# Attention in a transformer kernel on Trainium2: the order in which own and context keys are projected, and the block's order on every engine

## The chip, the cores and the metric

One core of one Trainium2 chip. The metric is the device time of one execution in microseconds (us), slowest core, lower is better. Differences of about 0.3% are the least that a measurement of this kernel tells from none.

## The reference, cut to what matters

The whole program is a two-layer transformer: cross attention, feed-forward, cross attention, feed-forward. The change touches the first attention only. For 8 batches of 256 positions:

```
xn = layernorm(x)                                  # 512 wide
q  = rms_norm(xn @ wq)      -> 16 heads of 128, rotated (rope)
k  = rms_norm(xn @ wk)      ->  4 key heads of 128, rotated
kc = rms_norm(ctx @ wk_ctx) ->  4 key heads of 128, not rotated
v  = xn @ wv ; vc = ctx @ wv_ctx
p  = softmax(q . [kc ; k] / sqrt(128), causal on the own part)
x  = x + (p . [vc ; v]) @ wo
```

Each key head serves 4 query heads. "Own" keys and values come from x, "context" ones from ctx_2048.

## The kernel before, in words

Attention is 64 blocks (`NBLK`). Block i is batch i // 8, key head i // 2 % 4 and query tile i % 2 (128 rows): 4 query heads against 384 keys in an even block and 512 in an odd one (256 of the context and the own ones up to the diagonal). So each key head is a pair of an even and an odd block, and each batch is 8 blocks. Numbers are kept to fp32 accuracy by splitting them into a high and a low plane (`kT[0]`, `kT[1]`; `planes[:,0]`, `planes[:,1]`) and by three products of planes.

Keys and values are made in 64 units, one per block, two blocks ahead: block i projects unit i + 2. A unit is either own or context for one key head (`unit`, L125). In the kernel before, apart from the first pair, the context unit is the even one and the own unit the odd one. The projection lands in a PSUM bank (`kv_bank`: `quad[:, 3]` for even units, `bK` for odd ones) and its keys go round the engines:

- own unit: PE projects (`pe_kv`, L393) -> ACT copies the raw keys out (`act_k_raw`, L592) and sums their squares (`act_k_sq`, L584) -> POOL rotates them (`pool_k_rope`, L1066 to L1068, `pool_k_add`, L1074) and takes the root (`pool_rs`, L1059) -> ACT scales (`act_k_scale`, L600) -> PE transposes back into the same bank (`pe_k_turn`, L405) -> ACT writes the high plane (`act_k_hi`, L624) -> DVE the low plane (`dve_k_lo`, L837) -> the scores of the next pair may start (`pe_s`, L449 to L451, waits for `kt_lo` at head 0).
- context unit: the same without the rotation; ACT scales straight out of the bank (`act_k_n`, L661), L626 and L839 write the planes.
- values: `act_v_hi` (L635) and `dve_v_lo` (L848), one block later.

Five instruction streams are written out by hand, and every engine runs its own list strictly in order: `pe_step`, `act_step`, `dve_step`, `pool_step` and the SP queue's loop in `sp_program`. Semaphores (`wait_ge`) tie them. There is no planner; the order within a block is what these functions say. In a block before:

- PE: scores of heads 0, 1; projection of unit i + 2 (24 matmuls); scores of heads 2, 3; transposed queries of block i + 1 (`pe_q_turn`, L433); queries of block i + 2 (12 matmuls, L421); probabilities times values of block i - 1 in three parts (`pe_pv`, L479), with `pe_k_turn(i + 2)` among them.
- DVE: per head the masked scores (`dve_ev`, L904) and the low plane of the probabilities (`dve_p_lo`, L891); the reciprocal of the sums (`dve_ri`, L912, twice); `dve_o_lo` (L939), `dve_v_lo`, `dve_q_lo` (L884), and at the end `dve_k_lo(i + 2)` and the rotation of the queries `dve_q(i + 2)` (L876 to L878).
- ACT: the exponentials (`act_exp`, L687, and a small scaling L692 after each second one), `act_q_sq` (L645), `act_q_hi` (L653) and the steps of the units above.
- POOL: the high plane of the probabilities (`pool_norm`, L1087, four times), `pool_q_add` (L1080), the steps of the units.
- SP: the transposing DMAs of the probability planes (L302), the store of the output.

Once per batch new input is brought in ("the turn", block i % 8 == 6): the context tiles are split (`act_c_hi`, L566, `act_c_square`, L667, `pool_c_lo`, L1046; at the end of block 4 of the batch), x is loaded (`sp_x`, L244), its statistics taken (`dve_ln_a`, L812 to L816, at the end of block 5), rooted (`pool_ln_rs`, L1052), applied (`dve_ln_b`, L822), transposed (`pe_x_turn`, L353) and split (`act_x_hi`, L574, `dve_x_lo`, L828), all three in block 6.

## Time and profile before

| | |
|---|---|
| median of 3 runs | 1596.91 us (1596.77 to 1601.76) |
| the profiled execution | 1596.18 us, of which its span 1594.9 us |
| attention's blocks in the trace | 27 to 905 us |
| mean granted TensorE clock | 0.964 of full speed |
| busy share of the span | PE 90%, DVE 72%, ACT 61%, POOL 45% |

Engines: PE is TensorE, PEld its weight loads, DVE VectorE, ACT ScalarE, POOL GpSimd, SP the DMA queue's engine. L405 is line 405 of the kernel. `out<-in` are the tiles that an instruction writes and reads. A wait "A <- B" is time in which A sat idle until B released it. An instruction that follows another on its engine often starts a little before the other's shown end, so steps are counted from start to start.

### The profile page before, as it was taken

To read this page: it belongs to the slowest core of one execution; us is meant where nothing else is said; L and a number is where in the kernel's file an instruction comes from. 1 tells how busy PE (TensorE), PEld (TensorE's weight loads), DVE (VectorE), ACT (ScalarE), POOL (GpSimd) and SP (SyncE) were. 2 spreads that over 40 slices of the span, in tenths; PEclk is the share of its full clock that TensorE was granted. 3 is DMA by queue.
4 is the path that set the end of the run, shared out by engine and by line. 5 is a ranking of instruction groups with operands and counts; after the bars stand their busy time and mean duration, and the time that the engine had idled before them with its cause. 6 is when DMAs were issued, how large, how long until landed. Compare 5 with 4: busy or idle time off the path is not lost. (4 is left out here: it accounts for less than half of the span.)

```text
span 1594.9 us, 24891 instructions
## 1 busy us (share of the span) xinstructions
PE 1429.5 (90%) x7820; PEld 1046.0 (66%) x7820; DVE 1156.2 (72%) x2836; ACT 975.1 (61%) x2647; POOL 716.1 (45%) x809
## 2 busy tenths in 40 slices
PE   7888989888979898889888789999998899999988
PEld 5665767666767676667676456666666566666653
DVE  5677776767767777777778875655566888888774
ACT  6565665666656656666565674555554666667655
POOL 5456464555554655655655600000003455555444
PEclk9789999999999999999998989999999999999999
DMA  7334555545545555555488998878885401111000
GB/s 282 70 83 118 119 126 115 114 113 124 125 120 114 125 115 117 115 123 126 106 203 202 255 308 276 287 248 256 267 264 161 151 21 47 54 54 41 28 14 27
DMA packets 321892, 223.76 MB, mean 140 GB/s; under 512 B 276960, under 2 KB 277088, under 8 KB 320352
## 3 DMA queue, kind: packets, MB, share of 16 engines
q1 hardware_dynamic: 321760, 222.16, 52.4%
q8 instruction: 63, 1.03, 0.3%
q14 instruction: 69, 0.57, 0.1%
HBM read 113.05 MB, written 41.94 MB: 97 GB/s over the span
## 5 line engine op out<-in xcount | busy, mean ns | idle before, releaser
L891 DVE SCALAR_TENSOR_TENSOR planes<-E,small,planes 128x384 f16<-128x384 f32 (+1 forms) x256 | 210.8, 843 | 70.5 <-POOL planes L1087 69.0
L1087 POOL TENSOR_SCALAR planes<-E,small 128x384 f16<-128x384 f32 (+1 forms) x256 | 160.0, 637 | 159.1 <-DVE small L912 151.7
L421 PE MATMUL bank<-wq,xT 128*128 128x512 f32 x768 | 199.6, 409 | 9.3 <-ACT wq L559 9.1
L687 ACT ACTIVATE E<-E,small 128x384 f32<-128x384 f32 (+1 forms) x256 | 170.8, 675 | 51.1 <-DVE small L904 51.0
L904 DVE CUSTOM_DVE_ANT_0 E<-quad,mask,small 128x384 f32<-128x384 f32 (+1 forms) x256 | 169.2, 677 | 44.7 <-PE quad L451 44.6
L1300 PE MATMUL bank<-wq,ot 128*128 128x512 f32 x768 | 187.6, 403 | 9.9 <-DMA ot<-ot_scratch 5.6
L479 PE MATMUL bank<-PT,vv 128*128 128x512 f16 x672 | 177.9, 401 | 0.0
L1300 PEld LDWEIGHTS bank<-wq,ot 128*128 128x128 f32 x768 | 147.8, 193 | 44.3 <-DMA ot<-ot_scratch 6.1
L421 PEld LDWEIGHTS bank<-wq,xT 128*128 128x128 f32 x768 | 143.4, 194 | 39.2 <-issue 9.3
L1080 POOL TENSOR_TENSOR t<-t 128x512 f32<-128x512 f32 x64 | 84.7, 1324 | 172.3 <-DVE t L878 172.3
L1596 POOL TENSOR_TENSOR cl<-cl,fixed 128x1 f32<-128x1 f32 x16 | 8.8, 550 | 279.5 <-DVE cl L1480 279.5
L449 PE MATMUL quad<-kT,qT 128*128 128x384 f32 (+1 forms) x256 | 107.8, 421 | 26.9 <-DVE kT L837 23.6
L2482 POOL TENSOR_TENSOR bhw<-bh,lnw 128x512 f32<-128x512 f32 x64 | 81.7, 1277 | 82.0 <-DVE bh L2270 81.9
L479 PEld LDWEIGHTS bank<-PT,vv 128*128 128x128 f16 x672 | 63.0, 101 | 71.4 <-issue 24.2
L393 PEld LDWEIGHTS quad<-wkc,cT 128*128 128x128 f32 x720 | 99.1, 209 | 0.0
L393 PE MATMUL quad<-wkc,cT 128*128 128x256 f32 x720 | 99.0, 298 | 0.0
L451 PE MATMUL quad<-kT,qT 128*128 128x384 f32 (+1 forms) x256 | 97.4, 381 | 0.0
L450 PE MATMUL quad<-kT,qT 128*128 128x384 f32 (+1 forms) x256 | 97.4, 380 | 0.0
L393 PEld LDWEIGHTS bank<-wkv,xT 128*128 128x128 f32 x744 | 93.4, 189 | 2.5
L1059 POOL TENSOR_TENSOR small<-small,fixed 128x6 f32<-128x6 f32 (+2 forms) x65 | 89.0, 1370 | 12.3 <-ACT small L611 12.3
L393 PE MATMUL bank<-wkv,xT 128*128 128x256 f32 x744 | 94.3, 283 | 0.0
L645 ACT ACTIVATE junk_sq<-bank 128x128 bf16<-128x128 f32 x256 | 67.4, 279 | 37.2 <-DVE t L878 37.0
(313 smaller groups left out, 3304.1 us busy)
## 6 DMA issues: line engine op xcount, KB each, us to landing
ot_scratch<-OT SPq DMA_DIRECT2D x64, 512.0 KB, 2.7
ot<-ot_scratch SPq DMA_DIRECT2D x64, 512.0 KB, 5.3
wkv_f<-in_w SPq DMA_DIRECT2D x12, 512.0 KB, 5.0
wkc_f<-in_w SPq DMA_DIRECT2D x12, 512.0 KB, 6.3
wkv_f<-in_wg SPq DMA_DIRECT2D x11, 512.0 KB, 6.8
wkv_f<-in_wd SPq DMA_DIRECT2D x11, 512.0 KB, 6.9
wkv_f<-in_wu SPq DMA_DIRECT2D x10, 512.0 KB, 7.1
stg<-in_ctxT SPq DMA_DIRECT2D x16, 256.0 KB, 3.0
```

Source lines behind the costliest of these rows:

```text
L393: ins = pe.matmul(kv_bank(u)[:, t * 256:t * 256 + 256], src[i][:, k, t * 128:t * 128 + 128], w[j][:, g, k, :], start=(n == 0), stop=(n == 11))
L421: ins = pe.matmul(bQ[:], xT[p][:, k, qt * 128:qt * 128 + 128], wq[j][:, g, k, :], start=(part == 0 and k == 0), stop=(part == 2 and k == 3))
L449: pe.matmul(bank[:, 0:n], qh, kh, start=True, stop=False)
L450: pe.matmul(bank[:, 0:n], ql, kh, start=False, stop=False)
L451: pe.matmul(bank[:, 0:n], qh, kl, start=False, stop=True).then_inc(f["s_mm"], 1)
L479: ins = pe.matmul(bO[:].rearrange("p (h q) -> p h q", h=4), vv[:, x, i // 2 % 2, kt, :], heads[:, y, :, kt, :], start=(part == 0 and kt == ...
L687: act.activation(p, p, ACT.Exp, bias=nm[:, i % 2, h:h + 1], scale=-1.0, accum_out=sm[:, i % 2, h:h + 1]).then_inc(f["s_exp"], 1)
L891: dve.scalar_tensor_tensor(plane(i, 1, h), E[:, h, 0:width(i)], ri[:, i % 2, h:h + 1], plane(i, 0, h), ALU.mult, ALU.subtract).then_inc(f[ ...
L904: dve.tensor_tensor_reduce(E[:, h, 0:n], bank_s(i, h)[:, 0:n], mask[:, 512 - n:512], scale=rs6[:, (i + 1) % 2, 2 + h:3 + h], scalar=3.0e38 ...
L1059: pool.tensor_tensor(rs6[:, e % 2, c], ve6[:, c], half[:, c], ALU.pow).then_inc(f["n_rs"], 1)
L1087: pool.tensor_scalar(plane(i, 0, h), E[:, h, 0:width(i)], ri[:, i % 2, h:h + 1], 1.0, ALU.mult, ALU.mult).then_inc(f["p_n"], 1)
L1300: ins = pe.matmul(y_bank(n)[:], ot[:, c % 4, i, k * 128:k * 128 + 128].bitcast(F32R), wo[j][:, g, k, :], start=(g == 0 and k == 0 and q == ...
```

## The change

Units: in all batches the own unit is now the even one (projected in even blocks) and the context unit the odd one, except for the first key head of batches 1 to 7, whose own unit needs the new x and stays odd (`unit`). `own_before` counts own units, since they no longer alternate. The own unit's second half of the work (`act_k_scale`, `pe_k_turn`, `act_k_hi`, `dve_k_lo`, and `act_v_hi`, `dve_v_lo`) moves from its own block to the next, odd one, and stands there right behind the scores of heads 2 and 3. In odd blocks the context unit's `pe_k_turn` follows the first part of `pe_pv`. On DVE `dve_q(i + 2)` and, in odd blocks, `dve_k_lo(i + 2)` stand ahead of `dve_p_lo(i, 3)`. At the turn, the statistics of x move from block 5 to block 6, the split of the context from the end of block 4 to the middle of block 5, x's loads from block 4 to block 5, and in block 7 the projection comes ahead of all scores. The weights of groups 1 to 3 are loaded and split with the own ones first. No arithmetic is added or taken away.

```diff
--- before.py
+++ after.py
@@ -125,18 +125,22 @@
     def unit(u):
 
 
-        bg, own = divmod(u, 2)
-        return bg, 1 - own if bg == 0 else own
+        bg, n = divmod(u, 2)
+        return bg, n if bg and bg % 4 == 0 else 1 - n
+
+    def own_before(u):
+
+        return sum(unit(w)[1] for w in range(u))
 
     def piece_of(p):
 
 
-        g, j = divmod(p, 4)
-        return g, (j + 1) % 4 if g == 0 else j
+        g, n = divmod(p, 4)
+        return g, ((1, 0, 2, 3) if g else (1, 2, 3, 0))[n]
 
     def pieces(g, j):
 
-        return 4 * g + (j - 1) % 4 + 1 if g == 0 else 4 * g + j + 1
+        return 4 * g + ((1, 0, 2, 3) if g else (1, 2, 3, 0)).index(j) + 1
 
     def piece(p):
 
@@ -314,7 +318,7 @@
         sp_w(0, "wkc")
         sp.dma_start(mask[:], a["mask"]).then_inc(f["mask_in"], 16)
         for g in range(1, 4):
-            for src in ("wkc", "wkv", "wq"):
+            for src in ("wkv", "wkc", "wq"):
                 sp_w(g, src)
         sp_c(2)
         sp_c(3)
@@ -330,14 +334,13 @@
                     for x in range(2):
                         sp_p_turn(i, half, x)
                         sp_last(i, 1 + 2 * half + x)
+                        if b + 1 < NB and r == 5 and half != x:
+                            sp_x(2 * b + 2 + half)
             elif i == NBLK:
                 sp_last(i, 4)
             if b + 1 < NB and r == 6:
                 sp_c(2 * b + 4)
                 sp_c(2 * b + 5)
-            if b + 1 < NB and r == 4:
-                sp_x(2 * b + 2)
-                sp_x(2 * b + 3)
 
 
 
@@ -495,22 +498,29 @@
 
     def pe_step(i):
         turn = i % 8 == 6 and i + 2 < NBLK
+        ahead = i % 8 == 7
+        if ahead:
+            pe_kv(i + 2, 0)
+            pe_kv(i + 2, 1)
         pe_s(i, 0)
         pe_s(i, 1)
         if i == 0:
             pe_q(1, 2)
-        pe_kv(i + 2, 0)
-        pe_kv(i + 2, 1)
+        if not ahead:
+            pe_kv(i + 2, 0)
+            pe_kv(i + 2, 1)
+        pe_s(i, 2)
+        pe_s(i, 3)
+        if i % 2:
+            pe_k_turn(i + 1)
         if turn:
+            for part in range(3):
+                pe_pv(i - 1, part)
             pe_x_turn(2 * (i // 8) + 2)
             pe_x_turn(2 * (i // 8) + 3)
-        pe_s(i, 2)
-        pe_s(i, 3)
-        if turn:
-            pe_pv(i - 1, 0)
-            pe_pv(i - 1, 1)
+            pe_scale(i)
         pe_q_turn(i + 1)
-        if scaled(i):
+        if scaled(i) and not turn:
             pe_scale(i)
         if i == 60:
             pe_w1_sum()
@@ -520,12 +530,10 @@
             ffn["pe_y"](0, 1)
         if not turn:
             pe_pv(i - 1, 0)
-            if i % 2 == 0:
-                pe_pv(i - 1, 1)
-        pe_k_turn(i + 2)
-        if i % 2:
+            if i % 2:
+                pe_k_turn(i + 2)
             pe_pv(i - 1, 1)
-        pe_pv(i - 1, 2)
+            pe_pv(i - 1, 2)
         if i == 62:
             pe.wait_ge(f["q_sq"], NBLK)
             ffn["pe_y"](0, 0)
@@ -562,7 +570,7 @@
         b, t = divmod(c, 2)
         sem, n = c_in(c)
         act.wait_ge(sem, n)
-        after(act, f["kv_mm"], 8 * b - 1)
+        after(act, f["kv_mm"], 8 * b)
         act.copy(cT[0][:, :, t * 128:t * 128 + 128],
                  stg[:, c % 2, :].rearrange("p (k n) -> p k n", k=4)).then_inc(f["c_hi"], 1)
 
@@ -589,12 +597,13 @@
             return
         act.wait_ge(f["kv_mm"], u + 1)
         after(act, f["kt_mm"], u)
+        after(act, f["k_rope"], own_before(u))
         act.copy(kn, kv4(u)[:, 0]).then_inc(f["k_raw"], 1)
 
     def act_k_scale(u):
         if u >= NU or not unit(u)[1]:
             return
-        act.wait_ge(f["k_rope"], u // 2 + 1)
+        act.wait_ge(f["k_rope"], own_before(u) + 1)
         act.wait_ge(f["n_rs"], u + 1)
         for t in range(2):
             ins = act.activation(ka[:, t], ka[:, t], ACT.Copy, scale=rs6[:, u % 2, t:t + 1])
@@ -656,7 +665,8 @@
         if u >= NU or unit(u)[1]:
             return
         act.wait_ge(f["n_rs"], u + 1)
-        after(act, f["kt_mm"], u)
+        after(act, f["k_rope"], own_before(u))
+        after(act, f["kt_mm"], u - unit(u - 1)[1])
         for t in range(2):
             ins = act.activation(kn[:, t], kv4(u)[:, 0, t], ACT.Copy, scale=rs6[:, u % 2, t:t + 1])
         ins.then_inc(f["k_n"], 1)
@@ -722,21 +732,30 @@
         if i == 0:
             act_w_hi(6)
         act_o(i - 2)
+        if i % 2 == 0 and i:
+            act_v_hi(i + 1)
         if i:
-            act_v_hi(i + 1)
             act_q_sq(i + 1)
         if 1 <= i <= 4:
             act_w_hi(2 * i + 6)
+        if i % 8 == 7:
+            act_k_raw(i + 2)
         act_exp(i, 0)
         act_exp(i, 1)
         if i == 0:
             act_q_sq(1)
-        act_k_raw(i + 2)
+        if i % 2:
+            act_k_scale(i + 1)
+        if i % 8 != 7:
+            act_k_raw(i + 2)
         act_k_sq(i + 2)
         act_ve(i + 2)
-        if turn:
-            act_x_hi(2 * (i // 8) + 2)
-            act_x_hi(2 * (i // 8) + 3)
+        if i % 8 == 5 and i + 3 < NBLK:
+            for m in (2 * (i // 8) + 2, 2 * (i // 8) + 3):
+                act_c_hi(m)
+                act_c_square(m)
+        if i % 2:
+            act_k_hi(i + 1)
         act_last(i, 0)
         act_exp(i, 2)
         act_k_n(i + 2)
@@ -745,18 +764,21 @@
             act_w_hi(7)
         elif i <= 4:
             act_w_hi(2 * i + 7)
+        if turn:
+            act_x_hi(2 * (i // 8) + 2)
+            act_x_hi(2 * (i // 8) + 3)
+        if i % 2:
+            act_v_hi(i + 1)
         act_q_hi(i + 1)
         if i == 0:
             act_v_hi(0)
             act_v_hi(1)
-        act_k_scale(i + 2)
-        act_k_hi(i + 2)
+        if i % 2:
+            if i % 8 == 7:
+                act_k_scale(i + 2)
+            act_k_hi(i + 2)
         if i in (1, 3):
             act_w_square(2 + i // 2)
-        if i % 8 == 4 and i + 4 < NBLK:
-            for m in (2 * (i // 8) + 2, 2 * (i // 8) + 3):
-                act_c_hi(m)
-                act_c_square(m)
         act_last(i, 1)
         act_last(i, 2)
 
@@ -947,35 +969,38 @@
             dve_w(5)
             dve_q(1)
         if turn:
+            dve_ln_a(2 * (i // 8) + 2)
+            dve_ln_a(2 * (i // 8) + 3)
+        dve_o_lo(i - 2)
+        if i % 2 == 0 and i:
+            dve_v_lo(i + 1)
+        dve_ri(i, 0)
+        if turn:
             dve_ln_b(2 * (i // 8) + 2)
             dve_ln_b(2 * (i // 8) + 3)
-        dve_o_lo(i - 2)
-        if i:
-            dve_v_lo(i + 1)
-        dve_ri(i, 0)
         if i == 0:
             dve_w(6)
         dve_last(i, 0)
         dve_ev(i, 2)
+        if i % 2:
+            dve_k_lo(i + 1)
+        dve_p_lo(i, 0)
+        dve_ev(i, 3)
+        dve_p_lo(i, 1)
+        if i % 2:
+            dve_v_lo(i + 1)
+        if 1 <= i <= 4:
+            dve_w(2 * i + 6)
+        dve_ri(i, 1)
         if turn:
             dve_x_lo(2 * (i // 8) + 2)
             dve_x_lo(2 * (i // 8) + 3)
-        dve_p_lo(i, 0)
-        dve_ev(i, 3)
         if scaled(i):
             dve_scale(i)
-        dve_p_lo(i, 1)
-        if 1 <= i <= 4:
-            dve_w(2 * i + 6)
-        dve_ri(i, 1)
         dve_q_lo(i + 1)
         if i == 0:
             dve_w(7)
         dve_p_lo(i, 2)
-        dve_p_lo(i, 3)
-        if i % 8 == 5 and i + 3 < NBLK:
-            dve_ln_a(2 * (i // 8) + 2)
-            dve_ln_a(2 * (i // 8) + 3)
         if scaled(i):
             dve_unscale(i)
         if i == 0:
@@ -983,11 +1008,13 @@
             dve_v_lo(1)
         if 1 <= i <= 4:
             dve_w(2 * i + 7)
-        dve_k_lo(i + 2)
+        dve_q(i + 2)
+        if i % 2:
+            dve_k_lo(i + 2)
+        dve_p_lo(i, 3)
         if i == 16:
             dve_co()
         dve_last(i, 1)
-        dve_q(i + 2)
 
     def dve_co():
 
@@ -1061,8 +1088,7 @@
     def pool_k_rope(u):
         if u >= NU or not unit(u)[1]:
             return
-        pool.wait_ge(f["k_raw"], u // 2 + 1)
-        after(pool, f["k_rope"], u // 2)
+        pool.wait_ge(f["k_raw"], own_before(u) + 1)
         pool.tensor_tensor(kb[:, :, 0:64], kn[:, :, 64:128], tab[:, 3, :, 0:64], ALU.mult)
         pool.tensor_tensor(kb[:, :, 64:128], kn[:, :, 0:64], tab[:, 3, :, 64:128], ALU.mult)
         g_.did(pool.tensor_tensor(ka, kn, tab[:, 2, :, :], ALU.mult))
@@ -1105,24 +1131,33 @@
         pool.tensor_tensor(lo, loaded, hi.bitcast(F32), ALU.subtract).then_inc(f["wo_lo"], 1)
 
     def pool_step(i):
+        turn = i % 8 == 6 and i + 2 < NBLK
         pool_q_add(i + 1)
+        if i % 8 == 7:
+            pool_k_rope(i + 2)
         pool_norm(i, 0)
         pool_norm(i, 1)
-        pool_k_rope(i + 2)
+        if turn:
+            pool_ln_rs(2 * (i // 8) + 2)
+            pool_ln_rs(2 * (i // 8) + 3)
+        if i % 8 != 7:
+            pool_k_rope(i + 2)
         pool_rs(i + 2)
-        pool_k_add(i + 2)
-        if scaled(i):
+        if i % 8 == 7:
+            pool_k_add(i + 2)
+        if i % 8 == 5 and i + 3 < NBLK:
+            pool_c_lo(2 * (i // 8) + 2)
+            pool_c_lo(2 * (i // 8) + 3)
+        if scaled(i) and not turn:
             pool_scale(i)
         pool_norm(i, 2)
         pool_norm(i, 3)
+        if scaled(i) and turn:
+            pool_scale(i)
+        if i % 8 != 7:
+            pool_k_add(i + 2)
         if i >= 57:
             pool_wo(i - 57)
-        if i % 8 == 4 and i + 4 < NBLK:
-            pool_c_lo(2 * (i // 8) + 2)
-            pool_c_lo(2 * (i // 8) + 3)
-        if i % 8 == 5 and i + 3 < NBLK:
-            pool_ln_rs(2 * (i // 8) + 2)
-            pool_ln_rs(2 * (i // 8) + 3)
 
     def pool_program():
         pool_ln_rs(0)
```

## Rows read from the trace of the kernel before

**Rows 1.** The waits of the whole program: who waited for whom, us in total, times, longest.

```profile
PE bank L405 <- ACT kk L600: 79.4, 31, 4.4
...
PE quad L449 <- DVE kT L837: 23.6, 25, 2.5
```

**Rows 2.** Windows: length, busy of PE, PEld, DVE, ACT, POOL (instructions), PEclk, DMA share, GB/s.

```profile
398.88:409.80 10.92, 10.91 (x66) 8.93 (x67) 7.77 (x20) 7.14 (x29) 4.88 (x6) 1.00 0.55 129
409.80:423.43 13.63, 11.60 (x66) 8.73 (x64) 10.15 (x23) 8.67 (x31) 8.44 (x10) 1.00 0.48 110
434.36:451.54 17.18, 11.61 (x66) 8.74 (x64) 12.51 (x29) 11.02 (x38) 11.82 (x14) 1.00 0.61 141
558.97:586.58 27.61, 24.69 (x145) 19.47 (x146) 20.84 (x50) 16.16 (x60) 15.93 (x21) 0.98 0.48 110
480.64:506.32 25.68, 23.66 (x130) 18.78 (x130) 18.06 (x43) 16.25 (x60) 13.35 (x16) 0.95 0.53 113
```

**Rows 3.** Timeline (start us, us, engine, line, operation, count) of PE, block 27.

```profile
411.38 3.04 PE L393 MATMUL bank<-wkv,xT 128*128 128x256 f32 x24
...
415.64 0.60 PE L433 MATMUL bank<-fixed,t 128*128 128x128 f32 x4
...
418.85 0.82 PE L479 MATMUL bank<-PT,vv 128*128 128x512 f16 x3
421.28 0.44 PE L405 MATMUL bank<-fixed,kk 128*128 128x128 f32 x2 [1.61 <-ACT kk L600]
```

**Rows 4.** Timeline of ACT in block 27.

```profile
410.77 0.47 ACT L635 ACTIVATE vv<-quad,small 128x256 f16<-128x256 f32 x1
...
418.14 0.20 ACT L692 ACTIVATE small<-small 128x2 f32<-128x2 f32 x1
...
421.76 0.37 ACT L624 CAST kT<-bank 128x256 fp32r<-128x256 f32 x1 [0.53 <-PE bank L405]
```

**Rows 5.** Timeline of DVE in block 27 and at the start of block 28.

```profile
410.23 0.68 DVE L876 TENSOR_TENSOR t<-bank,tab 128x512 f32<-128x512 f32 x1
...
411.49 0.74 DVE L904 CUSTOM_DVE_ANT_0 E<-quad,mask,small 128x512 f32<-128x512 f32 x1
...
415.84 0.75 DVE L891 SCALAR_TENSOR_TENSOR planes<-E,small,planes 128x512 f16<-128x512 f32 x1
...
418.38 0.17 DVE L912 RECIPROCAL small<-small 128x2 f32<-128x2 f32 x1 [0.46 <-ACT small L692]
...
421.20 1.83 DVE L891 SCALAR_TENSOR_TENSOR planes<-E,small,planes 128x512 f16<-128x512 f32 x2 [1.66 <-POOL planes L1087]
422.96 0.41 DVE L837 TENSOR_TENSOR kT<-bank,kT 128x256 fp32r<-128x256 f32 x1
423.30 0.68 DVE L876 TENSOR_TENSOR t<-bank,tab 128x512 f32<-128x512 f32 x1
```

**Rows 6.** Timeline of POOL in block 27.

```profile
420.49 1.35 POOL L1087 TENSOR_SCALAR planes<-E,small 128x512 f16<-128x512 f32 x2
```

**Rows 7.** Timeline of ACT at the start of block 29 and in block 30.

```profile
434.26 0.61 ACT L566 CAST cT<-stg 128x512 fp32r<-128x512 f32 x1
...
436.80 0.67 ACT L699 ACTIVATE OT<-bank,cl 128x512 fp32r<-128x512 f32 x1
...
458.05 1.05 ACT L574 CAST xT<-bank 128x512 fp32r<-128x512 f32 x2
```

**Rows 8.** Timeline of DVE at the end of block 29 and in block 30.

```profile
449.06 0.68 DVE L812 BATCH_NORM_STATS2 small<-stg 128x6 f32<-128x512 f32 x1
...
451.07 0.41 DVE L837 TENSOR_TENSOR kT<-bank,kT 128x256 fp32r<-128x256 f32 x1
...
453.73 1.11 DVE L822 TENSOR_SCALAR stg<-stg,small 128x512 f32<-128x512 f32 x2
...
459.22 1.28 DVE L828 TENSOR_TENSOR xT<-bank,xT 128x512 fp32r<-128x512 f32 x2
```

**Rows 9.** Timeline of POOL at the end of block 29.

```profile
451.23 0.56 POOL L1052 TENSOR_TENSOR small<-small,fixed 128x1 f32<-128x1 f32 x1 [0.44 <-DVE small L816]
```

## The prediction

> **What bounds the kernel now.** The busy shares name PE (90%), so the first view to read is what PE waits for [rows 1]. Two rows carry the attention stage: 31 waits for the scaled own keys (ACT L600), 79.4 us together, and 25 waits of the scores for the keys' low plane (DVE L837), 23.6 us. Both belong to the own unit, whose keys go through all four engines in the last block before they are needed. The windows [rows 2] show where: block 26 (even) takes 10.92 us with PE busy 10.91, block 27 (odd) 13.63 us with PE busy 11.60. Even blocks are bound by PE, odd ones by the keys' chain. Block 29, before the turn, takes 17.18 us at the same PE work. The turn's pair, 38 and 39, takes 27.61 us. So about 103 us could go, if nothing took the waits' place. Whether something does is read in the order of DVE and ACT in an odd block, since every engine keeps its list.
>
> Below, times in block 27 count from its first score at 409.80.
>
> **Even blocks.** The two transposes of a unit's keys leave PE (0.44 us long after a stall [rows 3]; I take 0.25 of PE's time), and PE has no gap to fill: 10.67 us instead of 10.92. POOL gets the rotation there, some 2.5 us before the high planes of heads 2 and 3. That makes the block's last low planes later, but the next block's scores don't wait for them, and the transposing DMAs have most of a block of slack. I cost it at nothing; if that cover went, the next masking would start late.
>
> **Odd blocks, the chain as it will be.** What was at the end is now in the middle.
> - PE's own-key transposes stand where the queries' stood, at 415.64, which is 5.84. From such a transpose to the high plane's copy takes 0.48 (421.28 to 421.76 [rows 3, 4]): 6.32. The copy is 0.37, with a handover of 0.04: DVE's low plane starts at 6.73 and holds DVE for 0.34 (422.96 to 423.30 [rows 5]): 7.07.
> - Only then comes the low plane of head 0, which stood at 415.84, i.e. 6.04 [rows 5]. It, the masking of head 3, its exponential and the scaling L692 behind it are now 1.03 later: L692 at 8.34 [rows 4] goes to 9.37.
> - Before, the reciprocal followed L692 at once (418.38, 8.58 [rows 5]). Now DVE's list has the values' low plane first, and that waits for ACT's high plane, which stands behind L692: 0.1, a copy of 0.47 [rows 4] with 0.04, and 0.39 of DVE (its twin on the keys is 0.41 long). That is 1.0: reciprocal at 10.37.
> - POOL's high planes of heads 2 and 3 follow 0.26 later, 10.63; before, they were held back by the rotation until 420.49, 10.69 [rows 6]. So all that the rotation's departure frees is used up by the two inserted steps.
> - Low plane of head 2 after 0.71 (420.49 to 421.20): 11.34. The two low planes took 1.76 until the keys' one began [rows 5]; a lone one is 0.75 long, 0.67 from start to start, so the first took 1.09. Next 12.43.
> - Then the queries' rotation, 1.26 (410.23 to 411.49 [rows 5]), and now the context keys' low plane at 13.69. From there to the next score 0.47 (422.96 to 423.43): **14.16** against 13.63.
>
> PE meanwhile is done at about 11.5 (its work from 418.85 on, 9.05, is nine matmuls and two transposes, 2.3 us). Its two waits have become one of 2.6 us at the first score of the next pair. The context unit's transposes find their keys ready. Sum of a plain pair: +0.53 - 0.25 = +0.28 us.
>
> **Block 29 and its like (six of them).** The statistics leave the end of DVE's list, 2.0 us straight ahead of the keys (449.06 to 451.07 [rows 8]). The context's four ACT operations, 2.54 us (434.26 to 436.80 [rows 7]), now stand ahead of the own keys' high plane: they start at about 5.5 and end at 8.05 where 6.32 was possible, +1.73. Block: 14.16 + 1.73 = 15.9 against 17.18. With the even one -1.5 us per pair.
>
> **The turn (seven).** In block 30 DVE now takes the statistics (2.0) where it took the normalisation (1.11 [rows 8]). Its first reciprocal comes at about 5.0. POOL does two high planes (1.4 with the start), then the roots of 0.56 [rows 9], DVE the normalisation from 7.0 to 8.05, and only then the masking of head 2. The exponentials of heads 2 and 3, behind it, are through at about 10.6 (estimate: 2.5 us after the masking, as there is one low plane and one exponential between). ACT's high planes of x follow them (two in 1.05 [rows 7]) and DVE's low ones (1.28 [rows 8]): 12.5. PE must have these before the queries' transposes, since they share a bank, and it runs out of other work at 9.5: the 10.67 of an even block, less the 3.2 of the queries (415.64 to 418.85 [rows 3]), and 2.2 for x and the scales (24.69 of PE in the turn's pair, 22.51 in blocks 26 and 27 [rows 2]), make 9.6. That is a new stall of some 3.1 us. Transposes and queries (3.2) and the projection of block 31, now first, 2.9 (411.38 for 3.04, less its overlap [rows 3]), follow: scores of block 31 at 18.7. That block then walks like an odd one, except that the projection is done: it saves about 2.0, 12.2. Sum 30.9 against 27.61: +3.3 us.
>
> **Queues.** SP's loads of x stand behind the transposes of block 29; they arrive at about 2 us into block 30 (3.0 us after issue), and the second statistics want them at 2.9. Cover, narrow; a miss would add to the turn. The weight loads change places only; blocks 0 to 5 wait for `wq`, which doesn't move.
>
> **Sum.** Twelve plain pairs +3.4; six with the context's split -9.2; seven turns +23.1; the first three and last four pairs, whose extra work (weights, sums) I don't follow, at the plain price +2.0. Together +19.3 on the profiled execution's 1596.2: **1615.5 us**. That execution lies 0.7 below the median of 1596.9; I forecast 1615. Bounds of the unknowns: each odd block's chain holds some ten handovers, which I take to be right within 0.3 us, below or above: 32 times, 10 us. The turn's new stall lies between 0 (all of it hidden) and 4.5 (x late too).
>
> **A rule weighed.** POOL's root of the norms (L1059) and the low plane of head 0 will overlap at 7.1. In the Trainium skill, SBUF — State Buffer, "Who interferes with whom", a VectorE instruction with two SBUF inputs and a GpSimd one that reads SBUF block each other for a whole instruction. The 1.09 for the first low plane beside POOL's L1087 agrees with it. By the rule the overlap with L1059 would add 0.1 per odd block, 3 us in all; my sum leaves it out.
>
> **Rivals.**
> - *PE's clock falls in every odd block.* Now block 27 has 2.03 us of idle PE in two parts, the longer 1.61 [rows 2, 3], at clock 1.00. Pair 38 and 39 has 2.92 (27.61 less 24.69 busy), and pair 32 and 33, which also follows a turn, shows 0.95 and takes 25.68 instead of 24.55 [rows 2], +1.13. A single wait of 2.6 us lies nearer to 2.9 than to 1.6. If it falls after each of some 18 to 25 odd blocks: +20 to +28, about 1638. In the Trainium skill, TensorE: Matmul & The Clock Gate, "What's actually happening", the full clock is what recent activity earns, so a longer unbroken wait speaks against this change. Against it: the sum of idle time in a pair hardly changes. 0.15.
> - *The turn is hidden.* If x's planes are ready before PE runs dry, seven stalls of 3.1 us go: 1593.5. For it: ACT is busy for 16.16 of the turn's 27.61 us [rows 2], so there is room. Against: nothing in the new list lets x's high planes go ahead of the exponentials. 0.18; half of it would be measured as no change.
> - *Faster: the odd block is bound by PE.* Place: the reciprocal of heads 2 and 3 in an odd block. If it comes at 7.8 instead of 10.4, the low plane of the keys is done by 11.1 and PE goes on at 11.5: 2.6 us less in 18 odd blocks, 1568. It beats the kernel before as soon as the reciprocal comes before about 9.3, on the plain pairs and with the turn as costed. It would need the own keys' transposes ready to be subtracted before head 2 is masked, at 5.4; PE issues them at 5.84. 0.10, part of it at a smaller gain.
> - *The low plane of head 2 loses the 0.42 us that it spends beside POOL* (1.09 less 0.67), because the lists now meet elsewhere. Then 31 x 0.42 less: 1602. Against it: both high planes still follow each other on POOL there. 0.07.
>
> **From these to the numbers.** Forecast 0.50, the rest as above. Faster by over 0.3% (under 1592.1; 0.3% is about what a measurement of this kernel tells from no change): the PE-bound case and half of the hidden turn, 0.18. Within: the rest of the hidden turn and a little of the others, 0.15. Slower: 0.67. Range 1591 to 1636: it leaves out the PE-bound case, the lowest part of the hidden turn and the clock's worst, some 0.2. The forecast's own range is 1605 to 1625.
>
> **What will show it.** In the waits: "PE bank L405 <- ACT kk L600" down from 79.4 to under 25 (block 31's kind alone), and the scores' wait for the low plane up from 23.6 to 60 or 80, now with L839. In the windows: even blocks 10.7, odd ones 14.2, block 29's kind 15.9, the turn's pair near 31 with a gap of 3 us ahead of L433. In DVE's timeline of an odd block: a wait ahead of L848 and L912 at 10.4. PEclk 1.00 in plain pairs. I am wrong if odd blocks come out near 11.5 (the chain is shorter than walked), if the gap ahead of L433 is missing in the turn, or if plain pairs show a clock below 1.

## The result, and the profile after

The changed kernel takes 1656.91 us (median of four runs, 1655.94 to 1658.66), the kernel before 1598.06 in the same comparison (four runs): ratio 1.0366, 95% interval 1.0344 to 1.0387. That is some 59 us more where I forecast 18 more, above my range of 1591 to 1636. The direction was right, the size not.

Where the time is shows in one window for each kernel, from the start of the span to the first score of block 62. Columns as in [rows 2]. The kernel before, then the changed one:

```profile
0.00:888.07 888.07, 767.36 (x4222) 600.01 (x4222) 644.88 (x1461) 546.33 (x1960) 491.11 (x584) 0.95 0.56 131
```

```profile
0.00:946.79 946.79, 798.54 (x4223) 636.60 (x4223) 667.17 (x1463) 537.86 (x1960) 496.29 (x584) 0.91 0.51 122
```

Nearly all of the difference, 58.7 of the spans' 59.8 us, is in the attention stage. PE runs as many instructions (4222 and 4223) and is busy 31.2 us longer with them, at a granted clock that fell from 0.95 to 0.91. The rest, 27.5 us, is more idle time.

The waits of PE in the changed kernel, the counterparts of [rows 1] (its lines: scores L452 to L454, own-key transposes L408, queries' transposes L436):

```profile
PE quad L452 <- DVE kT L861: 83.1, 24, 5.8
...
PE bank L408 <- ACT kk L609: 26.6, 7, 3.8
...
PE bank L436 <- issue: 16.1, 7, 2.4
```

The first two rows moved as forecast, both a little further up than said: the wait for the scaled own keys fell from 79.4 to 26.6 (forecast "under 25"), the scores' wait rose from 23.6 to 83.1 ("60 or 80"), in longer single waits. The third is the new gap of the turn.

The windows of blocks 26, 27, 29, 30 and 31 of the changed kernel, as in [rows 2]:

```profile
426.08:438.30 12.22, 12.22 (x65) 10.19 (x65) 8.76 (x20) 6.21 (x26) 7.74 (x10) 0.86 0.43 102
438.30:452.45 14.15, 11.56 (x67) 9.01 (x66) 10.37 (x25) 9.37 (x34) 6.03 (x7) 1.00 0.52 117
464.66:481.07 16.41, 11.57 (x67) 9.01 (x65) 10.95 (x25) 11.53 (x40) 8.55 (x9) 1.00 0.52 118
481.07:502.22 21.15, 18.71 (x104) 16.24 (x105) 13.71 (x34) 9.25 (x38) 9.23 (x13) 0.84 0.36 81
502.22:516.11 13.89, 10.09 (x44) 6.34 (x42) 9.40 (x22) 6.60 (x22) 7.52 (x11) 0.85 0.55 142
```

The chain of the odd block, in DVE's timeline of block 27 (columns as in [rows 5]; the block's first score is at 438.30; L859 and L861 are the low planes of own and context keys, L913 the low planes of the probabilities, L898 to L900 the queries' rotation):

```profile
444.95 0.42 DVE L859 TENSOR_TENSOR kT<-quad,kT 128x256 fp32r<-128x256 f32 x1 [0.56 <-ACT kT L633]
...
448.19 0.48 DVE L870 SCALAR_TENSOR_TENSOR vv<-quad,small,vv 128x256 f16<-128x256 f32 x1 [0.82 <-ACT vv L644]
448.59 0.15 DVE L934 RECIPROCAL small<-small 128x2 f32<-128x2 f32 x1
...
449.57 1.17 DVE L913 SCALAR_TENSOR_TENSOR planes<-E,small,planes 128x512 f16<-128x512 f32 x1 [0.22 <-POOL planes L1113]
450.67 0.68 DVE L898 TENSOR_TENSOR t<-bank,tab 128x512 f32<-128x512 f32 x1
...
451.93 0.47 DVE L861 SCALAR_TENSOR_TENSOR kT<-bank,small,kT 128x256 fp32r<-128x256 f32 x1
452.32 1.60 DVE L913 SCALAR_TENSOR_TENSOR planes<-E,small,planes 128x512 f16<-128x512 f32 x1
```

Counted from 438.30: own keys' low plane 6.65 (walked 6.73), reciprocal 10.29 (10.37), low plane of head 2 at 11.27 (11.34), rotation 12.37 (12.43), context keys' low plane 13.63 (13.69). The waits in brackets are the two inserted steps: DVE waits for the own keys' high plane, and, ahead of the reciprocal, for the values' high plane. What the walk did not price is the last row: 1.60 us for an operation that takes 0.75 in [rows 5].

PE's side of the same block and of the turn:

```profile
452.45 0.45 PE L452 MATMUL quad<-kT,qT 128*128 128x384 f32 x1 [2.59 <-DVE kT L861]
...
494.54 0.78 PE L436 MATMUL bank<-fixed,t 128*128 128x128 f32 x4 [2.43 <-issue]
494.97 4.54 PE L424 MATMUL bank<-wq,xT 128*128 128x512 f32 x12
...
512.99 0.69 PE L408 MATMUL bank<-fixed,kk 128*128 128x128 f32 x2 [3.80 <-ACT kk L609]
```

There is one wait of 2.59 us at the scores, as walked (2.6), and the clock falls behind it: 1.00 in the window of block 27, 0.86 in those of the even blocks on either side. The queries' projection behind the turn's gap takes 4.54 us; in an odd block, at full clock, 2.98.

### The profile page after: what moved, and what is told of

Its sections match the earlier page's. It is cut to its first block and busy times, and to the rows that moved or that the text cites. A ratio compares the mean times of both kernels' runs of the same rounds, so it can differ in the third digit from the quotient of the medians.

```text
span 1654.7 us, 24817 instructions
## 1 busy us (share of the span) xinstructions
PE 1456.5 (88%) x7777; PEld 1082.5 (65%) x7820; DVE 1178.2 (71%) x2836; ACT 966.8 (58%) x2647; POOL 722.5 (44%) x809
## 5 line engine op out<-in xcount | busy, mean ns | idle before, releaser
L913 DVE SCALAR_TENSOR_TENSOR planes<-E,small,planes 128x384 f16<-128x384 f32 (+1 forms) x256 | 233.4, 912 | 17.9 <-POOL planes L1113 15.1
L424 PE MATMUL bank<-wq,xT 128*128 128x512 f32 x768 | 208.7, 423 | 10.4 <-ACT wq L567 6.8
L452 PE MATMUL quad<-kT,qT 128*128 128x384 f32 (+1 forms) x256 | 109.5, 428 | 84.2 <-DVE kT L861 83.1
L424 PEld LDWEIGHTS bank<-wq,xT 128*128 128x128 f32 x768 | 150.4, 203 | 41.9 <-issue 6.9
L482 PE MATMUL bank<-PT,vv 128*128 128x512 f16 x672 | 171.1, 397 | 2.2 <-DVE vv L870 2.2
L1106 POOL TENSOR_TENSOR t<-t 128x512 f32<-128x512 f32 x64 | 95.1, 1486 | 112.8 <-DVE t L900 112.8
L452 PEld LDWEIGHTS quad<-kT,qT 128*128 128x128 f32 x256 | 52.6, 205 | 108.7 <-DVE kT L861 95.4
L482 PEld LDWEIGHTS bank<-PT,vv 128*128 128x128 f16 x672 | 63.0, 102 | 81.0 <-issue 22.8
L709 ACT ACTIVATE OT<-bank,cl 128x512 fp32r<-128x512 f32 x64 | 44.1, 689 | 118.6 <-PE bank L482 110.5
L1086 POOL TENSOR_TENSOR small<-small,fixed 128x6 f32<-128x6 f32 (+2 forms) x65 | 98.8, 1520 | 7.3 <-ACT small L620 7.2
L454 PE MATMUL quad<-kT,qT 128*128 128x384 f32 (+1 forms) x256 | 101.9, 398 | 0.0
L453 PE MATMUL quad<-kT,qT 128*128 128x384 f32 (+1 forms) x256 | 101.5, 396 | 0.0
L396 PEld LDWEIGHTS quad<-wkv,xT 128*128 128x128 f32 x552 | 91.9, 249 | 0.0
L396 PE MATMUL quad<-wkv,xT 128*128 128x256 f32 x552 | 90.3, 334 | 0.0
```

The source lines that it names most:

```text
L396: ins = pe.matmul(kv_bank(u)[:, t * 256:t * 256 + 256], src[i][:, k, t * 128:t * 128 + 128], w[j][:, g, k, :], start=(n == 0), stop=(n == 11))
L424: ins = pe.matmul(bQ[:], xT[p][:, k, qt * 128:qt * 128 + 128], wq[j][:, g, k, :], start=(part == 0 and k == 0), stop=(part == 2 and k == 3))
L452: pe.matmul(bank[:, 0:n], qh, kh, start=True, stop=False)
L453: pe.matmul(bank[:, 0:n], ql, kh, start=False, stop=False)
L454: pe.matmul(bank[:, 0:n], qh, kl, start=False, stop=True).then_inc(f["s_mm"], 1)
L482: ins = pe.matmul(bO[:].rearrange("p (h q) -> p h q", h=4), vv[:, x, i // 2 % 2, kt, :], heads[:, y, :, kt, :], start=(part == 0 and kt == ...
```

## Experiments

The theory after this reading: the chain is as walked, and what the forecast lacks is (a) PE's clock, and (b) time in the turn. The rival: the even blocks are slower for a reason of their own (the late low planes), and the clock is only its mark. A block starts at its first score; sums over pairs below are differences of such starts.

### Filling PE's waits: fill_waits and before_filled

Constant matmuls stand in PE's waits, into a bank that the next scores overwrite, so nothing computed hangs on them. In the changed kernel 10 stand ahead of the first score of even blocks (20 in the turn's, none behind it), 11 ahead of the turn's queries and 15 ahead of block 31's own-key transposes. In the kernel before, 7 or 13 ahead of L405 in odd blocks, and 9 ahead of the turn's first score.

```diff
+    def pe_fill(i, n):
+        after(pe, f["s_ev"], 4 * i - 2)
+        for _ in range(n):
+            pe.matmul(bank_s(i, 0).rearrange("p (k n) -> p k n", k=4), mem["idh"][:],
+                      mem["idh"][:].unsqueeze(1).broadcast_to((128, 4, 128)), start=True, stop=True)
...
         if h == 0:
+            if i % 2 == 0 and i % 8:
+                pe_fill(i, 20 if i % 8 == 6 else 10)
```

> The changed kernel with matmuls on constants in PE's waits (10 ahead of the first score of even blocks, 20 in the turn's block, 11 ahead of the queries' transposes of the turn, 15 ahead of the keys' transposes of block 31's kind); their results are overwritten. The engines' waits stay. Theory 1 (the extra over the walked chain is PE's clock at 1.2 GHz after the longer single waits): even blocks fall from 12.2 to 10.7 us, the turn's block from 21.2 to 18 to 19, PEclk near 1.00 in plain pairs, total 1600 to 1615 us. Theory 2 (VectorE comes late into the even blocks, because its last low plane takes 1.6 us beside GpSimd's L1106): even blocks stay at 12.2, total about 1657.

> The kernel before with matmuls on constants in its own waits (7 ahead of the own keys' transposes of odd blocks, 13 in those of blocks 29's and 31's kind, 9 ahead of the turn's first score), overwritten like the others. It is the control for fill_waits: if the filling does nothing but hold PE's clock, the plain pairs stay at 24.5 us, PEclk there at 1.00, and only the falls at the turns go, about 1 to 3 us per batch: 1582 to 1592 us. If filling also helps or hurts in another way, plain pairs change.

Measured: 1619.73 us (four runs; 1600 to 1615 was expected), ratio to the kernel before 1.0114 (1.0083 to 1.0145); the filled kernel before 1586.54 (four), ratio 0.9918 (0.9886 to 0.995). Windows of blocks 26, 27, 30 and 31 of the changed kernel, filled:

```profile
414.28:424.99 10.71, 10.71 (x64) 8.68 (x65) 8.76 (x19) 6.20 (x26) 7.72 (x10) 1.00 0.49 117
424.99:439.14 14.15, 13.72 (x77) 9.99 (x75) 10.60 (x25) 9.36 (x34) 6.01 (x7) 1.00 0.52 117
466.24:485.50 19.26, 18.71 (x115) 14.38 (x116) 13.63 (x34) 9.12 (x38) 9.07 (x13) 1.00 0.40 89
485.50:499.38 13.88, 11.94 (x58) 7.38 (x56) 9.39 (x22) 7.30 (x24) 7.51 (x11) 1.00 0.56 142
```

and of the kernel before, filled, for blocks 26, 29, 30 and 31 (27 takes 13.63):

```profile
394.81:405.71 10.90, 10.90 (x67) 8.90 (x67) 7.75 (x20) 7.12 (x29) 4.89 (x6) 1.00 0.56 130
430.23:447.40 17.17, 16.35 (x87) 10.87 (x85) 12.51 (x29) 11.01 (x38) 11.81 (x14) 1.00 0.61 140
447.40:460.07 12.67, 12.67 (x82) 10.70 (x83) 8.98 (x25) 7.98 (x30) 7.06 (x11) 1.00 0.30 79
460.07:474.99 14.92, 14.40 (x79) 9.99 (x77) 11.86 (x26) 8.55 (x31) 8.86 (x11) 1.00 0.56 138
```

With the waits filled the clock is 1.00 in each of these windows, and the even block is 10.71, the forecast's 10.67, with the late low planes still in place. The odd block stays at 14.15. So the 1.5 us of each even block are the clock's, and the rival falls for the plain blocks. In the Trainium skill, TensorE: Matmul & The Clock Gate, "What's actually happening", the full clock is what recent activity earns; these windows agree, as PE's activity is all that the fill adds.

The two filled kernels are also the fair comparison of the rest. Up to block 62 the filled change takes 911.47 us, the filled kernel before 877.32: +34.2 without the clock. Against their own filled versions the change loses 946.79 - 911.47 = 35.3 to the clock, the kernel before 888.07 - 877.32 = 10.8: **+24.6 by the clock**. 34.2 and 24.6 make the 58.7, but for rounding. Each of the four numbers is from one execution; the medians of the two filled kernels lie 33.2 apart (1619.73 less 1586.54), so the split is good to a few us.

### Which half of the change: last_plane_back and before_with_new_tail

The change swaps the order of the units and reorders DVE's tail. The first kernel keeps the swap (and all that the change does at the turn) and puts the tail back; the second is the kernel before with the new tail alone (in all blocks). "The swap alone" below is the first one, read in plain pairs.

```diff
@@ last_plane_back, on the changed kernel, dve_step
-        dve_q(i + 2)
+        dve_p_lo(i, 3)
         if i % 2:
             dve_k_lo(i + 2)
-        dve_p_lo(i, 3)
+        dve_q(i + 2)
@@ before_with_new_tail, on the kernel before, dve_step
         dve_p_lo(i, 2)
-        dve_p_lo(i, 3)
...
+        dve_q(i + 2)
         dve_k_lo(i + 2)
+        dve_p_lo(i, 3)
...
-        dve_q(i + 2)
```

> The changed kernel with VectorE's tail as it was: low planes of heads 2 and 3, then the context keys' low plane, then the queries' rotation. So the swap of the units alone. Theory 1 (VectorE's list sets the next score; the clock goes by the length of the single wait): the keys' plane starts 0.6 us earlier in each odd block, 14.15 to 13.5 us; the wait is 2.0 instead of 2.6 us, and as the kernel before had 1.6 at full clock and 2.9 at a fall, the clock falls seldom: total 1595 to 1625 us. Theory 2 (the order of the tail is of no weight, the swap does it all): 1650 us or more.

> The kernel before with the changed tail on VectorE alone (low plane of head 2, the queries' rotation, the keys' low plane, low plane of head 3; statistics ahead of it). Theory 1: the own keys' plane starts 0.6 us later in odd blocks, 13.63 to 14.2 us; the second of its two waits grows from 0.6 to 1.2 us; even blocks 10.9 where the clock holds: total 1612 to 1630 us. Theory 2 (this tail is a gain, as the swap only hides): below 1597 us.

Measured: 1634.91 us (four runs), ratio 1.0224 (1.0192 to 1.0255), and 1610.28 (six), ratio 1.0073 (1.0045 to 1.0102). The first is above the 1595 to 1625 expected, the second just under its 1612 to 1630. Blocks 26 and 27 of the first, then block 27 of the second (its block 26 takes 10.93, clock 1.00):

```profile
420.05:432.25 12.20, 12.20 (x64) 10.17 (x65) 8.48 (x20) 6.20 (x26) 8.12 (x10) 0.86 0.48 112
432.25:445.81 13.56, 11.56 (x67) 9.00 (x65) 10.13 (x24) 9.37 (x34) 5.33 (x6) 1.00 0.49 113
```

```profile
416.94:431.00 14.06, 11.61 (x65) 8.72 (x63) 11.52 (x24) 9.01 (x32) 8.73 (x11) 1.00 0.58 115
```

The tail costs a plain odd block 0.6 us with the swap (14.15 against 13.56) and 0.4 without (14.06 against 13.63): the rotation, 1.26, stands ahead of the keys, and the last low plane, 0.7, leaves. The swap alone leaves the odd block where it was; only its wait is in another place. PE's timeline shows what that does, first with the swap alone, at the starts of blocks 26 and 34, with the window of block 34 beneath, then with the tail alone:

```profile
420.05 0.45 PE L452 MATMUL quad<-kT,qT 128*128 128x384 f32 x1 [1.97 <-DVE kT L861]
...
530.55 0.45 PE L452 MATMUL quad<-kT,qT 128*128 128x384 f32 x1 [2.00 <-DVE kT L861]
```

```profile
530.55:541.26 10.71, 10.71 (x64) 8.68 (x65) 8.49 (x20) 6.20 (x26) 7.91 (x10) 1.00 0.65 128
```

```profile
428.26 0.44 PE L405 MATMUL bank<-fixed,kk 128*128 128x128 f32 x2 [1.44 <-ACT kk L600]
431.00 0.45 PE L449 MATMUL quad<-kT,qT 128*128 128x384 f32 x1 [1.01 <-DVE kT L837]
```

With the tail alone PE is idle for 2.45 us of the block in two parts, and the clock stays at 1.00. With the swap alone it is idle for only 2.0, in one part, and the clock falls behind some of these waits (block 26, 0.86) and not behind others (block 34, 1.00). So the sum of the waits is not what counts. The longest single one is the better guide, yet it does not decide the single case. In these traces, of the even blocks of plain pairs and of pairs with block 29's kind that follow such a wait, none of 11 had lost the clock after 1.4 to 1.6 and 1.0 us in two parts, 3 of 12 after a single 2.0, and all 12 after a single 2.6 in the changed kernel; but only 9 and 8 of 12 after the same 2.6 in roots_first and turn_keys_early below. Where the wait stands is not what does it: before_keys_mid, below, has it ahead of the transposes and loses the clock behind 1.96 us in blocks 12 and 36. In the kernel before, a wait of 2.91 us in the block that follows the turn's leaves the next block below 1.00 in five cases of seven.

### The position of the keys' low plane: keys_before_planes and before_keys_mid

If the chain is DVE's list and nothing else, the context keys' low plane can stand right behind that of the queries, before DVE waits for POOL's high planes. The second kernel does the like to the kernel before.

```diff
@@ keys_before_planes, on the changed kernel, dve_step
         dve_q_lo(i + 1)
+        if i % 2:
+            dve_k_lo(i + 2)
...
-        if i % 2:
-            dve_k_lo(i + 2)
@@ before_keys_mid, on the kernel before, dve_step
         dve_p_lo(i, 2)
+        if i % 2:
+            dve_k_lo(i + 2)
         dve_p_lo(i, 3)
...
-        dve_k_lo(i + 2)
+        if not (i % 2):
+            dve_k_lo(i + 2)
```

> The changed kernel with the context keys' low plane in odd blocks right behind the queries' low plane, ahead of the low plane of head 2 and of the queries' rotation. Theory 1 (VectorE's list is what holds the next score; PE's clock follows the wait): the keys' plane starts at 11.1 instead of 13.4 us of the block, odd blocks 14.15 to 11.6, even blocks 12.2 to 10.7 since the wait and with it the slow clock goes; 18 pairs x 4 us less, about 1585 us with the turn unchanged. Theory 2 (the transposes or ACT's high plane come late too): odd blocks stay above 13, total above 1630.

> The kernel before with the own keys' low plane in odd blocks between the low planes of heads 2 and 3 (and so ahead of the statistics in block 29's kind). Theory 1 (its order decides the shorter of the two waits): plain odd blocks 13.63 to 13.05 us, block 29's kind 17.18 to about 15, of which the next block takes some back; total 1575 to 1588 us. Theory 2 (the low planes that are now late hold the transposing DMAs and with them PE): no change, 1597 us.

Measured: 1602.22 us (ten runs), ratio 1.0016 (1.0001 to 1.003), and 1581.75 (four), ratio 0.9891 (0.9847 to 0.9936). About 1585 was expected of the first, 1575 to 1588 of the second. Blocks 27 and 30 of the first, then blocks 27 and 29 of the second:

```profile
415.85:427.37 11.52, 11.52 (x68) 9.01 (x66) 9.46 (x23) 8.70 (x32) 6.53 (x8) 1.00 0.56 126
...
452.78:476.24 23.46, 20.06 (x104) 16.66 (x105) 15.03 (x38) 9.23 (x38) 10.02 (x14) 0.79 0.43 94
```

```profile
405.20:418.50 13.30, 11.35 (x65) 8.73 (x63) 10.19 (x23) 8.17 (x30) 8.45 (x10) 1.00 0.48 110
...
429.43:445.13 15.70, 12.56 (x65) 9.22 (x64) 11.40 (x24) 10.31 (x36) 10.96 (x12) 0.91 0.71 139
```

One operation of 0.47 us moved, and the odd block is bound by PE: 11.52 long, PE busy 11.52, and the next even block is at full clock. It takes 54.7 us off the changed kernel. So the swap does shorten the path of the context's keys (they are ready before 11.5). The new tail throws that away by letting them stand behind the low plane of head 2 and the rotation, the old one by letting them stand behind both low planes. The kernel only draws level with the one before, as the turn gets worse: its block takes 22.7 us on average for 20.9, and block 30, shown above, is the longest of the seven. What now stands behind the keys in DVE's list, two low planes and the rotation, runs over into the turn's block. The statistics of x start there at 3.86 us instead of 2.76, and the low plane of the output (`dve_o_lo`, L961), which is behind them, ends 1.1 us or more later (in block 30 at 7.04 instead of 5.51). PE's product with the values (L482) waits for it:

```profile
459.08 0.74 DVE L961 SCALAR_TENSOR_TENSOR OT<-bank,cl,OT 128x512 fp32r<-128x512 f32 x1
```

```profile
459.92 2.75 PE L482 MATMUL bank<-PT,vv 128*128 128x512 f16 x12 [0.54 <-issue]
```

In all seven turns of this kernel the product starts 0.1 us after that low plane ends; in the changed kernel it never waits there. In plain even blocks the same overrun costs nothing.

On the kernel before, where the own keys come last in any order, the like edit gives 0.3 to 0.7 us per plain odd block and 2.3 on average in block 29's kind (14.84 for 17.18; block 29, shown, is the longest of the six at 15.70).

### The turn: roots_first and turn_keys_early

What the turn's gap waits for is read without the clock in DVE's list of the filled kernel (block 30 starts at 466.24; there L925 is the low plane, L938 the masking, L856 the normalisation of x):

```profile
466.11 1.60 DVE L925 SCALAR_TENSOR_TENSOR planes<-E,small,planes 128x512 f16<-128x512 f32 x1
467.63 0.61 DVE L938 CUSTOM_DVE_ANT_0 E<-quad,mask,small 128x384 f32<-128x384 f32 x1
...
473.73 1.16 DVE L856 TENSOR_SCALAR stg<-stg,small 128x512 f32<-128x512 f32 x2 [1.80 <-POOL small L1091]
474.81 0.61 DVE L938 CUSTOM_DVE_ANT_0 E<-quad,mask,small 128x384 f32<-128x384 f32 x1
```

Next, POOL's rotation (L1106) at the same place in the changed kernel, block 30 starting at 481.07, and ACT's raw copy of the next own keys in block 31:

```profile
480.71 1.27 POOL L1106 TENSOR_TENSOR t<-t 128x512 f32<-128x512 f32 x1 [1.89 <-DVE t L900]
```

```profile
505.43 0.37 ACT L601 COPY kk<-bank 128x256 f32<-128x256 f32 x1 [3.35 <-issue]
```

The order is the one walked, each step half a microsecond late: reciprocal (471.77) at 5.53 (5.0), normalisation at 7.49 (7.0), masking of head 2 at 8.57 (8.05), end of x's low planes (479.31) at 13.07 (12.5). The delay is there in the first two rows: the low plane beside POOL's L1106 takes 1.60, and masking starts at 1.39. In block 31 PE's transposes of the context keys of unit 32 stand at 504.97, and ACT's raw copy of the own keys of unit 33 (L601), which reuses the buffer that they read, comes behind them, after 3.35 us idle. Behind it stand the exponentials and the keys' rotation, and at 512.99 PE itself waits 3.80 us for those keys.

Two edits, one for each of the two:

```diff
@@ roots_first, on the changed kernel, pool_step
-        pool_norm(i, 0)
-        pool_norm(i, 1)
         if turn:
             pool_ln_rs(2 * (i // 8) + 2)
             pool_ln_rs(2 * (i // 8) + 3)
+        pool_norm(i, 0)
+        pool_norm(i, 1)
@@ turn_keys_early, on the changed kernel, pe_step
-        if i % 2:
+        if i % 2 and i % 8 != 7:
             pe_k_turn(i + 1)
...
             pe_scale(i)
+            pe_k_turn(i + 2)
         pe_q_turn(i + 1)
```

> The changed kernel with GpSimd's roots of the layer norm ahead of the high planes of heads 0 and 1 in the turn's block. Theory 1 (the turn's wait comes from VectorE's normalisation, behind the roots, behind the high planes): the normalisation starts some 1.7 us earlier, the wait ahead of the queries' transposes falls from 2.4 to about 1, seven times: 10 to 20 us less in all, 1637 to 1647 us. Theory 2 (the split of x is held by ACT's exponentials in any case): under 4 us less.

> The changed kernel with PE's transposes of the context keys of unit i + 2 of the turn (unit 8, 16, ...) moved from block 31's kind into the turn, ahead of the queries' transposes. Theory 1 (in block 31's kind ACT's raw copy of the own keys waits for these transposes, and both first exponentials wait behind it; my walk had missed that): the copy comes right behind the projection, the exponentials 1.8 us earlier, PE's wait for L609 falls from 3.8 to 2 us, block 31's kind from 13.9 to 12.2: 12 us less, 1640 to 1647 us. Theory 2 (something else holds the raw copy): no change, 1657.

Measured: 1634.09 us (four runs), ratio 1.0214 (1.0178 to 1.025), and 1629.41 (four), ratio 1.0187 (1.0157 to 1.0218): both faster than expected (1637 to 1647 and 1640 to 1647). Blocks 26, 28 and 30 of the first, then block 31 of the second:

```profile
418.66:429.35 10.69, 10.69 (x65) 8.65 (x65) 8.76 (x19) 6.20 (x26) 7.69 (x10) 1.00 0.48 115
443.50:455.72 12.22, 12.22 (x64) 10.19 (x65) 8.76 (x20) 6.19 (x26) 7.73 (x10) 0.86 0.43 103
...
472.12:490.43 18.31, 17.11 (x105) 15.05 (x105) 13.78 (x34) 9.35 (x38) 9.51 (x13) 0.91 0.42 94
```

```profile
496.44:508.53 12.09, 9.91 (x41) 6.05 (x40) 9.39 (x22) 6.71 (x22) 7.52 (x11) 0.88 0.66 163
```

With the transposes of unit 32 a block earlier, block 31 takes 12.09, the 12.2 of the forecast: the 1.7 us were this wait. With the roots first the turn's block takes 18.3 to 20.1, on average 19.2 where it had 20.9. By the medians the two gain 22.8 and 27.5 us over the changed kernel; the profiled executions, which the windows are from, gain less, 15.6 and 23.6. In these, 12.4 and 18.5 are in the seven turn pairs (243.7 us together, now 231.3 and 225.2), and 8.9 and 7.5 in the twelve plain pairs, which neither edit touches (314.7, now 305.8 and 307.2): the clock didn't fall in some of them. Elsewhere a part is lost again.

### Together: three_mends and five_mends

The first is the changed kernel with the three edits (keys_before_planes, roots_first, turn_keys_early). The second adds to it, on ACT, the context's four operations behind the exponential of head 2 in block 29's kind, and in the turn the high planes of x ahead of the exponential of head 3:

```diff
-        if i % 8 == 5 and i + 3 < NBLK:
-            for m in (2 * (i // 8) + 2, 2 * (i // 8) + 3):
-                act_c_hi(m)
-                act_c_square(m)
...
         act_exp(i, 2)
+        if i % 8 == 5 and i + 3 < NBLK:
+            for m in (2 * (i // 8) + 2, 2 * (i // 8) + 3):
+                act_c_hi(m)
+                act_c_square(m)
         act_k_n(i + 2)
+        if turn:
+            act_x_hi(2 * (i // 8) + 2)
+            act_x_hi(2 * (i // 8) + 3)
         act_exp(i, 3)
```

> The changed kernel with the keys' plane ahead of the low planes, the roots first in the turn, and the turn's key transposes early. If the causes are separate: 1602 for the first alone, less 15 to 20 for the roots, less 12 for the transposes: 1565 to 1580 us, below the kernel before. If they only shift the same wait about: above 1595.

> The three mends and two more on ScalarE: in block 29's kind the split of the context behind the exponential of head 2 instead of ahead of the own keys' high plane, and in the turn the high planes of x ahead of the exponential of head 3. Theory 1 (in both places the one list order sets PE's wait): block 29's kind 14.7 to about 12.5 us, the turn's block about 0.8 us shorter, seven times each: 15 to 25 us under the three mends, 1550 to 1560 us. Theory 2 (x's loads, which stand behind block 29's planes on SP, then come too late): 1570 or more.

Measured: 1574.65 us (four runs), ratio 0.985 (0.9822 to 0.9878), and 1571.50 (four), ratio 0.982 (0.9788 to 0.9852). Blocks 30 and 31 of the first (its 29 takes 14.72), 29 and 30 of the second:

```profile
440.04:461.48 21.44, 19.17 (x106) 16.44 (x107) 15.10 (x38) 9.35 (x38) 10.49 (x14) 0.84 0.46 103
461.48:472.76 11.28, 9.07 (x41) 5.97 (x40) 7.98 (x19) 6.71 (x22) 7.20 (x10) 0.92 0.59 160
```

```profile
423.50:436.82 13.32, 11.81 (x67) 8.92 (x65) 10.17 (x23) 11.58 (x40) 9.51 (x10) 1.00 0.58 126
436.82:458.84 22.02, 17.61 (x106) 14.93 (x107) 15.00 (x38) 9.27 (x38) 10.54 (x14) 0.92 0.52 90
```

The three edits beat the kernel before by 1.5%, inside the 1565 to 1580 expected, but aren't shown to beat before_keys_mid, whose interval (0.9847 to 0.9936) overlaps theirs. In the turn they add up: the seven pairs take 223.6 us against 253.1 in keys_before_planes, 29.5 less, where the two edits took off 12.4 and 18.5 one by one. In the whole they do not: the three took off 54.7, 22.8 and 27.5 us, 105 in all, and together 82.3. In the traces the plain pairs take 270.6 us with the three and 269.2 with keys_before_planes alone, so what the other two gained there isn't gained again.

five_mends missed its 1550 to 1560. Of the two edits on ACT only the one in block 29's kind bears fruit (13.32 against 14.72, where 12.5 was expected). The turn's block grows from 20.7 to 21.7 us on average, and PE's idle time in it from 3.0 to 4.3. DVE's list shows why the high planes of x ahead of the exponential of head 3 do not help: the low planes of x stand behind the second reciprocal, and this waits for that exponential, which the edit made later. In block 30 of five_mends:

```profile
449.72 0.17 DVE L935 RECIPROCAL small<-small 128x2 f32<-128x2 f32 x1 [2.13 <-ACT small L703]
```

In three_mends that wait is 1.14 us. So the low planes of x end at 13.9 of the block instead of 13.3 in most of the turns, and the gap ahead of the transposes is 2.55 instead of 1.98. In two of the seven turns (22 and 46) the second statistics also wait for x's load, for 1.1 and 1.2 us, which was the rival's condition. The second kernel isn't shown to be faster than the first.

## Why the prediction failed on the size

| part | forecast, us | at full clock (filled kernels, summed over the pairs) |
|---|---|---|
| 12 plain pairs | +3.4 | 298.5 for 295.4: +3.1 |
| 6 pairs with block 29's kind | -9.2 | 162.6 for 168.5: -5.9 |
| 7 turn pairs | +23.1 | 232.1 for 193.2: +38.9 |
| before block 0, first three and last three pairs | +2.0 | 218.3 for 220.2: -1.9 |
| sum | +19.3 | 911.5 for 877.3: +34.2 |
| PE's clock | 0 | +24.6 |

- **The walk of the odd block, right.** 14.16 against 14.15, and each step within 0.1. That both transposes and values' planes step into DVE's list is in the brackets of L859 and L870. last_plane_back shows the step under it: without the new tail, 13.56.
- **The clock, the step that failed most.** The forecast set plain pairs at clock 1.00, so its sum has the clock at 0, and gave the rival 0.15, at +20 to +28. It measured +24.6, with a clock of 0.86 in the even blocks; a clock below 1 in plain pairs was one of the signs of being wrong. The reason I gave against it ("the sum of idle time in a pair hardly changes") was the error: waits of 1.61 and 0.41 became one of 2.59, and at an equal sum the longer single one lost the clock. The row to heed stood beside it: the pair behind a turn, at 0.95, follows a pair with some 2.9 of idle PE. Of the seven such pairs in that trace, five begin below 1.00 (0.90 to 0.92) and two at 1.00.
- **The turn, mis-sized by 2.3 us per pair** (5.6 for 3.3). 1.7 of it is block 31 (13.89 against 12.2): the walk had the projection first in that block and left ACT's list unwalked, in which the raw copy waits for the transposes that it overwrites. turn_keys_early puts it at 12.09. The other 0.56 (19.26 against 18.7) goes with the first step of the block, the masking half a microsecond late.
- **"I cost it at nothing" (the rotation and last low planes in the even block).** It holds in plain blocks, which take 10.71 with PE full. In the turn a late low plane lies on the path, though another one than I had in mind: that of head 3 of the odd block, which the new tail puts behind the keys' plane and so at the start of the turn's block, beside POOL's step of the queries' rotation (L1106, 1.27). It takes 1.60 us, and 0.74 where POOL does nothing. In the Trainium skill, SBUF — State Buffer, "Who interferes with whom", a VectorE instruction with two SBUF inputs and a GpSimd one that reads SBUF shut each other out for a whole instruction; the rows agree, as the plane is 0.85 longer over an overlap of 1.04 us (480.94 for 1.59, L1106 from 480.71 to 481.98). No run takes this overlap away, so its share of the 0.56 us is argued, not shown. I had weighed that rule at the low plane of head 0, which takes 0.74 and starts at 445.29, when POOL's root (L1086, 443.89 for 1.34) is over, and not at this one.
- **Block 29's kind, 0.5 short.** The wait for the context's four ACT operations was forecast at 1.73 over a plain block; it is 2.26 (16.41 less 14.15). The own keys' low plane comes at 8.34 instead of 6.65, which is 1.69 later and as walked. The rest is in the next step, the low plane of head 0, which takes 1.32 us instead of the 0.74 of block 27. The change has moved POOL's low planes of the context beside it, and the walk left POOL's list out there:

```profile
473.34 1.32 DVE L913 SCALAR_TENSOR_TENSOR planes<-E,small,planes 128x512 f16<-128x512 f32 x1
```

```profile
471.56 2.55 POOL L1073 TENSOR_TENSOR cT<-stg,cT 128x512 fp32r<-128x512 f32 x2
```

  With ACT's four operations moved behind the exponential, five_mends takes 1.4 off the block.
- **First and last pairs.** I gave them the plain price. The last three gained 5.8 (82.3 for 88.1). They take 81.7 us in before_with_new_tail and 89.8 in the kernel before, so the new tail alone gives it; how wasn't looked into.
- **The PE-bound rival (0.10) was nearer than I gave it credit for.** Its condition, an earlier reciprocal, did not come; but keys_before_planes reaches the same 11.5 us by another door, taking the keys out from behind it.

## What to carry to other kernels

Walk every engine's list through a moved step, the block behind it too: buffers that a moved reader frees late are waits on another engine. Moving a wait is not neutral even where its sum stays the same: waits of 1.44 and 1.01 us kept PE's clock, one of 2.0 lost it at times and one of 2.6 mostly. Filling it with constant matmuls shows in one run what part is the clock's. And where two steps swap places, the gain lands only if the list of the engine that finishes them is reordered to match: here one operation of 0.47 us, moved ahead of the low planes, decided some 55 us, and what it pushed back came out as a longer turn.
